# A landing buffer for the gathered tokens: GpSimd copies it to the rows that TensorE turns, and the first two gathers are issued back to back

## The reference

```python
def layer(x, mask, Wq, Wo, ffn):                      # x: 16 x 256 x 512 f32
    h = attention(x, mask, Wq, Wo)                    # 8 heads over 512 positions, rows h: 4096 tokens x 512
    logits = einsum('bsh,eh->bse', h, gate_w); probs = softmax(logits)
    top_w, top_i = top_k(probs, 2); top_w /= sum(top_w)            # 8 experts, 2 for each token
    g = einsum('bsh,ehi->besi', h, w_gate); u = einsum('bsh,ehi->besi', h, w_up)      # I = 352
    expert_out = einsum('besi,eih->besh', silu(g) * u, w_down)
    moe_out = einsum('besh,bse->bsh', expert_out, combine)          # combine: top_w at top_i, else 0
    shared_out = (silu(h @ sw_gate) * (h @ sw_up)) @ sw_down        # 1408 wide
    return x + moe_out + shared_out * sigmoid(h @ shared_gate_w)
```

## Time and profile before

| | |
|---|---|
| median of 3 timed runs | 1990.24 us (1988.90 to 1992.98) |
| the profiled execution | 2000.18 us, of which span 1998.40 us |
| granted TensorE clock, mean | 0.969 |
| TensorE busy in the span | 1887.1 us (94%) |
| VectorE / ScalarE / GpSimd busy | 982.0 / 735.2 / 665.2 us |

### The profile page before, as it was taken

One profiled execution on the slowest core, in us unless ns is written; L12 is line 12 of the kernel. 1 busy time (PEld: TensorE's weight loads), 2 busy tenths in 40 slices (PEclk: granted clock), 3 DMA queues, 4 the chain that ended last, 5 costly groups with the idle time before them and its releaser, 6 DMA issues. The chain is left out here.

```text
span 1998.4 us, 27812 instructions
## 1 busy us (share of the span) xinstructions
PE 1887.1 (94%) x9512; PEld 1382.3 (69%) x9513; DVE 982.0 (49%) x1605; ACT 735.2 (37%) x1432; POOL 665.2 (33%) x500
## 2 busy tenths in 40 slices
PE   4999999999999859799999999989999999999999
PEld 2444444445444347698988999968788888888887
DVE  3677777777777438432333323245523233333333
ACT  1566667666666622343333433331001010101010
POOL 3576776767775616311111111111101001010100
PEclk7899999999999969999999999989999999999999
DMA  6786767676765063433333232253503021211111
GB/s 123 113 134 102 116 100 131 102 116 99 134 91 76 22 217 108 152 117 117 117 117 117 73 119 77 79 184 90 170 31 95 22 84 31 73 42 63 42 43 42
DMA packets 117636, 193.89 MB, mean 97 GB/s; under 512 B 11856, under 2 KB 43600, under 8 KB 117552
## 3 DMA queue, kind: packets, MB, share of 16 engines
q1 hardware_dynamic: 106912, 157.93, 35.3%
q0 software_dynamic: 10640, 34.87, 6.0%
HBM read 99.40 MB, written 42.21 MB: 71 GB/s over the span
## 5 line engine op out<-in xcount | busy, mean ns | idle before, releaser
L382 DVE TENSOR_REDUCE maxcol<-ps_m 128x1 f32<-128x512 f32 x512 | 342.5, 684 | 180.4 <-PE ps_m L525 173.4
L321 ACT ACTIVATE e<-ps_e 128x512 f32<-128x512 f32 x512 | 297.4, 596 | 191.1 <-PE ps_e L520 190.3
L126 POOL TENSOR_TENSOR e<-e 128x2048 f32<-128x2048 f32 x64 | 225.1, 3517 | 99.1 <-ACT e L321 99.1
L1416 ACT ACTIVATE s_silu<-s_ps_g 128x512 f32<-128x512 f32 x77 | 46.0, 598 | 560.9 <-PE s_ps_g L1539 560.9
L1384 POOL DMA_INDIRECT s_chosen<-routed,s_slot_now x64 | 63.4, 991 | 565.8 <-DVE s_total L1470 555.2
L520 PE MATMUL ps_e<-qside,kside 98*128 98x512 f32 x512 | 241.8, 475 | 9.2 <-ACT e L321 7.4
L1495 DVE TENSOR_TENSOR s_h_f<-s_silu,s_ps_u 128x512 f32<-128x512 f32 x77 | 53.0, 688 | 394.2 <-PE s_ps_u L1539 365.8
L520 PEld LDWEIGHTS ps_e<-qside,kside 98*128 98x128 f32 x512 | 96.4, 189 | 213.1 <-ACT e L321 175.4
L525 PE MATMUL ps_m<-kside,qside 97*128 97x512 f32 x512 | 215.3, 424 | 17.7 <-DMA qside<-row_mask 14.2
L1054 DVE TENSOR_TENSOR e_h_lo<-e_ps_h,e_h_hi 128x256 fp32r<-128x256 f32 (+1 forms) x136 | 41.9, 350 | 222.3 <-ACT e_h_hi L869 222.3
L1551 PE MATMUL s_ps_y<-s_d_hi,s_h_hi 128*128 128x512 f32 x352 | 137.8, 392 | 2.5 <-DVE s_h_lo L1452 1.9
(11 more groups left out here) (241 smaller groups left out, 3919.3 us busy)
## 6 DMA issues: line engine op xcount, KB each, us to landing
routed<-keep_y SPq DMA_DIRECT2D x68, 256.0 KB, 2.0
kside<-q_hi SPq DMA_DIRECT2D x64, 256.0 KB
qside<-qm_hi SPq DMA_DIRECT2D x64, 256.0 KB
x_f<-in_x SPq DMA_DIRECT2D x16, 512.0 KB, 4.0
kside<-q_lo SPq DMA_DIRECT2D x32, 256.0 KB
qside<-qm_lo SPq DMA_DIRECT2D x32, 256.0 KB
attn<-xo SPq DMA_DIRECT2D x32, 256.0 KB, 3.9
keep_rows<-attn SPq DMA_DIRECT2D x8, 1024.0 KB, 5.6
```

The lines of the kernel that those rows point to most:

```text
L126: eng.tensor_tensor(into, into, e[k + 1][:, heads, :], ALU.add).then_inc(done, 1)
L321: act.activation(e[kb][:, g, :], ps_e[g % 2][:, :], ACT.Exp, scale=SCALE).then_inc(e_done, 1)
L382: dve.reduce_max(maxcol[par][:, g * KB + kb:g * KB + kb + 1], ps_m[g % 2][:, :], AX.X).then_inc(max_done, 1)
```

## The change

A second buffer of the same size, `landing`, and a second one-column tile, `first_now`, are added. Gather 0 goes straight to `rows`, with its own token column `first_now` and semaphore `first_in`. Gather 1 is issued right behind it, to `landing`. In the loop, GpSimd runs `take(j)`: it waits until gather j has landed and tile j-1's rows have been turned, copies `landing` to `rows` and raises `rows_done`; it then waits for that copy and issues gather j+1 to `landing`. So the data that TensorE turns comes from a copy, not from the DMA; `turn` waits for `rows_done` (for `first_in` at tile 0). The number of gathers is the same, 69; 68 copies of 128 x 512 f32 are added on GpSimd.

```diff
--- before.py
+++ after.py
@@ -586,8 +586,8 @@
     hi = [[sb(f"hi_{w}{n}", raw[k].shape, f32r) for k, w in enumerate("gud")] for n in range(2)]
     lo = [[sb(f"lo_{w}{n}", raw[k].shape, f32r) for k, w in enumerate("gud")] for n in range(2)]
     token_of = sb("token_of", [P, NCOL], u32)
-    now = sb("now", [P, 1], u32)
-    rows = sb("rows", [P, H], f32)
+    first_now, now = sb("first_now", [P, 1], u32), sb("now", [P, 1], u32)
+    rows, landing = sb("rows", [P, H], f32), sb("landing", [P, H], f32)
     x_hi, x_lo = sb("x_hi", [P, HT, ST], f32r), sb("x_lo", [P, HT, ST], f32r)
     silu, h_f = sb("silu", [P, I], f32), sb("h_f", [P, I], f32)
     h_hi, h_lo = sb("h_hi", [P, NI, ST], f32r), sb("h_lo", [P, NI, ST], f32r)
@@ -630,7 +630,7 @@
     row_hot, col_hot, token_hot, id_mm, ids_done = (sem(n) for n in ("row_hot", "col_hot", "token_hot", "id_mm", "ids_done"))
     base, consts, raw_in = sem("base"), sem("consts"), sem("raw_in")
     hi_done, lo_done = sem("hi_done"), sem("lo_done")
-    now_done, rows_in = sem("now_done"), sem("rows_in")
+    now_done, first_in, rows_in, rows_done = sem("now_done"), sem("first_in"), sem("rows_in"), sem("rows_done")
     t_mm, g_mm, half_u, u_mm, ht_mm, y_mm = (sem(n) for n in ("t_mm", "g_mm", "half_u", "u_mm", "ht_mm", "y_mm"))
     xhi_done, xlo_done = sem("xhi_done"), sem("xlo_done")
     silu_done, h_done, hhi_done, h_split = sem("silu_done"), sem("h_done"), sem("hhi_done"), sem("h_split")
@@ -797,21 +797,26 @@
         pool.wait_ge(bounds_done, 1)
         pool.wait_ge(ids_done, 1)
 
-        def gather(j):
-            pool.tensor_copy(now[:], token_of[:, bass.ds(j, 1)]).then_inc(now_done, 1)
-            if began(j):
-                alone(pool, t_mm, 2 * j, ids_done, 1)
+        def gather(j, into, by, landed):
+            pool.tensor_copy(by[:], token_of[:, bass.ds(j, 1)]).then_inc(now_done, 1)
             alone(pool, now_done, j + 1, ids_done, 1)
-            pool.indirect_dma_start(out=rows[:], out_offset=None, in_=attn,
-                                    in_offset=bass.IndirectOffsetOnAxis(ap=now[:, 0:1], axis=0)).then_inc(rows_in, 16)
-
-        gather(0)
+            pool.indirect_dma_start(out=into[:], out_offset=None, in_=attn,
+                                    in_offset=bass.IndirectOffsetOnAxis(ap=by[:, 0:1], axis=0)).then_inc(landed, 16)
+
+        def take(j):
+
+            pool.wait_ge(rows_in, 16 * j)
+            alone(pool, t_mm, 2 * j, ids_done, 1)
+            pool.tensor_copy(rows[:], landing[:]).then_inc(rows_done, 1)
+
+        gather(0, rows, first_now, first_in)
+        gather(1, landing, now, rows_in)
         total = tiles_in_all(pool)
-        with pool.Fori(0, total) as j:
-
-            pool.wait_ge(rows_in, 16 * (j + 1))
-            gather(j + 1)
-        pool.wait_ge(rows_in, 16 * (total + 1))
+        with pool.Fori(1, total) as j:
+            take(j)
+            alone(pool, rows_done, j, ids_done, 1)
+            gather(j + 1, landing, now, rows_in)
+        take(total)
 
     @block.scalar
     def _(act):
@@ -1132,7 +1137,10 @@
         pe.sem_inc(y_mm, 1)
 
         def turn(j):
-            pe.wait_ge(rows_in, 16 * (j + 1))
+            if began(j):
+                pe.wait_ge(rows_done, j)
+            else:
+                pe.wait_ge(first_in, 16)
             for a in range(2):
                 for m in range(HT // 2):
                     k = a * HT // 2 + m
```

## The result

| | before | after |
|---|---|---|
| median of the timed runs (11 each) | 1993.08 us | 1983.49 us |
| lowest to highest | 1988.90 to 1996.03 | 1977.83 to 1987.55 |
| the profiled execution | 2000.18 us | 1980.60 us |
| turn 0 to turn 68 in it | 479.2 us | 466.3 us |

A forecast was written before the change was run, and what follows sets the result against it. TensorE was taken to bound the expert stage, stopped by late gathers and slowed in clock after some stops. Gains 11.4 + 4.8 + 3.9 - 1.4 = 18.7 us, from 1990.24 to 1971.5 us; range 1965 to 1981.

The forecast's parts named there:

- slow tiles: Expert tiles at TensorE's lower clock after three of the six later stops: all three vanish, 3 x 1.6 = 4.8 us gained.
- the first two gathers: First tiles: early gather 1 removes the 5.69 us stop, a new 3 us stop and slow clock follow; gain 3.9 us.
- VectorE beside the copy: Next expert's weight splits on VectorE slowed by GpSimd's copy, once for each of seven experts: loss 1.4 us (0 to 3.6).
- The stops: Steady expert tiles: TensorE's six later waits for gathers vanish, 10.1 us plus 1.3 us lost around them, gain 11.4 us.
- the margin of 9.3 us: Steady tiles: time from a gather's issue to its needed landing with the new buffer, where 5.2 us were; covers 8.0 us gathers.
- nothing in that chain moves: Ordinary tile: the chain through h_lo to TensorE's weight load, with 0.79 us of slack, stays as it was.
- Rival 4: Every tile: the copy holds up VectorE's h_lo, 0.5 us over the slack, 34 us against a gain of 20; 2004 us, chance 0.07.
- Rival 1: First tiles: gather 2 passes the loads in 4 us, so turn 2 has no stop; 1965.5 to 1967 us, chance 0.14.
- Rival 2: Expert tiles: a stop stays at each expert, or only short stops go; gain 8 to 14, about 1979 us, chance 0.12.
- Rival 3: Timed runs: the stops could be the profiler's, so the time stays within 0.2%; chance 0.04.

The follow-up runs named there:

- e7: Changed kernel with new tensors allocated last, next stage's first loads moved to the second last expert, and the copy after h_lo: ratio 0.9934 to before, median 1977.06 us.
- e4: Changed kernel, with GpSimd also waiting for VectorE's h_lo of the same tile before its copy: ratio 0.9939 to the kernel before.
- e2: Changed kernel, with first_now and landing allocated behind all other tensors of the stage: ratio 0.9931 to the kernel before.
- e1: Kernel before, with first_now and landing allocated in their places but never used: ratio 1.0015 to the kernel before.
- e6: Kernel before, with only the 4-byte first_now allocated, unused: profiled only, ordinary tile 6.76 us, turn 0 to turn 68 476.1 us.
- e9: Kernel before, with both new tensors allocated unused, the first 64 bytes instead of 4: profiled only, ordinary tile 6.70 us, turn 0 to turn 68 477.9 us.
- e3: Changed kernel, with the next stage's first loads (2.6 MB) moved from the start of the tiles to the second last expert: ratio 0.9945 to the kernel before.
- e8: Changed kernel, with GpSimd waiting for turn 0 before it issues gather 1: ratio 0.9978 to the kernel before.

## Why the prediction was half right

The sign and the mechanism were right: the landing buffer takes the stops out. Wrong were three terms of the sum, which together are most of what is missing. In the means of the profiles (three before, two after), between turns 0 and 68:

| term | forecast | measured |
|---|---|---|
| stops at turns 13 to 48, with the loss around them | 9.8 | 9.6 |
| the stop at turn 5 | 1.6 | 0.6 |
| slow tiles | 4.8 | 2.6 |
| the first two gathers | 3.9 | 3.4 |
| VectorE beside the copy | -1.4 | -2.6 |
| the pace of TensorE | nothing | -3.2 |
| sum | 18.7 | 10.4 |

The timed medians give 9.6. How the right column comes about: without any stop turns 5 to 68 would have taken 57 x 6.70 + 6 x 7.05 = 424.2 us before, and e7, which has none there, takes 424.18. The three profiles have 436.4 in the mean, 12.2 more; 1.7 slow tiles of 1.56 us over their pace are 2.6 of that, and 9.6 are left for the stops. The changed kernel has 430.0, 5.8 over 424.2: 2.6 come back with e4 (the splits), 3.2 with e2 (the addresses). Turns 0 to 5 went from 40.0 to 36.0, of which 3.4 up to turn 4 and 0.6 from there to turn 5.

**The stops (11.4 us): right, but for one.** GpSimd's round was even shorter than reckoned (copy 0.61, not 0.9; gather issued 1.94 us after the turn, not 2.3). The step that failed here is the word "six": the margin of 9.3 us was worked out for a GpSimd that is on time. At expert 2's loads it was not. Gathers 2 and 3 had landed late, and a round of GpSimd that waits for its own gather takes 841.43 - 836.14 = 5.3 us (gather 4 to gather 5), so that it makes up only 1.5 us with each tile. Gather 5 was issued at 841.43, behind the first of expert 2's loads, and not at about 837.4, 1.94 us behind turn 3, and took 7.8 us. Turn 5 stopped 1.33 us in one profile and 0.52 in the other.

**The slow tiles (4.8 us): the term that was mis-sized.** I counted three of them in one execution and credited them as a fixed cost. In three profiles there were 3, 2 and 0, a mean of 1.7, or 2.6 us. The warning was in my own text: the profiled execution was 9.9 us above the timed median, and I carried the gain over to that median in full.

**The pace: a term that was missing, taken as nothing.** 3.2 us were lost (e2), because even the 4-byte tensor moves the operands of TensorE off their 64-byte starts (e1, e2, e6, e9). No rival held it; "nothing in that chain moves" looked at the order of instructions and not at where their tensors lie.

**VectorE beside the copy (loss 1.4): right, but too small.** The bound from the earlier trace rows, 0 to 0.51 each, held: at the same addresses a split tile takes 7.44 in the changed kernel and 7.01 to 7.03 in e1, and 7.46 in e2 against 7.05 before, 0.41 to 0.43 for each of six, the wait of 0.41 us in the rows above. With the copy moved away (e4) it came back, and the splits and the copy had their old lengths. The Trainium skill's rule ("GPSIMD Engine Reference", Key points: contention where VectorE has two SBUF inputs) puts the loss there too, and the trace of e4 agrees: 1.81 us without the copy beside it, against 2.23. Rival 4, the same in every tile, is refuted: in ordinary tiles h_lo keeps its 0.62 us, and with the addresses put right (e2) the period is 6.70. (Its written sum, 0.75 + 0.62 + 0.7, makes 2.07; the 1.3 that it goes on with is the copy's end at 1.51 less the 0.2 at which `h_lo` starts.)

**The start (3.9 us): near, and partly by luck.** Gather 1 came without a stop, and a new stop stood at turn 2: 2.59 us where 3.0 were forecast. Turn 2 comes 12.5 us after turn 0 (829.6 - 817.0 = 12.6 were forecast). But the 1.6 us that were taken off for a slow clock behind this stop did not come: the granted clock from turn 2 to turn 3 is 1.00 (826.12 to 834.83). What took their place is the stop at turn 3, "nothing, or under 1 us" in the forecast and 1.72 and 1.95 us in the two profiles. One error stood in for another.

Rival 1 (the first stop goes as well) is refuted by the 2.59 us, and e3 shows that even with the next stage's loads gone gather 2 takes 7.0 us. It did get through before the loads were over: it was copied at 825.45, and the DMA engines stayed full until about 834. Rival 2 had about the right size, a gain of 8 to 14, by the wrong mechanism: no stop stays at each expert. Rival 3 falls with the ratio: the timed runs gained what the means of the profiles gained.

## What to carry to other kernels

A second buffer is worth the waits of the slow gathers and no more; count those from several executions, since the length of a stop and what follows it (here zero to three slow-clock tiles, 0 to 5 us) change from one to the next. When a change adds even a four-byte tensor, ask what is allocated behind it: put new small tensors last, or pad them, and compare the period of an undisturbed tile before and after. A copy on GpSimd was free beside VectorE's operations with a PSUM input (`h_lo` 0.62 us with it and without), and belongs outside the stretch in which VectorE subtracts two SBUF tensors.

## What the runs showed of the hardware

- TensorE's pace depends on where its SBUF operands begin: 6.70 us for a tile of 40 matmuls and transposes with tensors at multiples of 64 bytes, 6.76 at 32 over it, the mean of ten tiles in a row the same within 0.005 us in all 14 profiles. The starts are my reading of compiled kernels, not of a trace. In the gate and down products the operands that moved are those of the LDWEIGHTS.
- Two stops of nearly the same length (1.98 and 2.02 us) were followed by an 8.31 us tile at a granted clock of 0.80 and by a 6.77 us tile at 1.00. Of 13 stops of 1.95 to 2.35 us 10 were followed by a slow tile, of 30 of 0.91 to 1.92 us none.
- A GpSimd copy of 128x512 f32 in SBUF took 0.61 us, and up to 1.09 beside two-input VectorE subtractions (minimum, median and maximum of 68 in ns; 1.32 at most in e3 and e8):

```profile
L810 POOL COPY e_rows<-e_landing x68: 610/612/1089, 816.3 to 1273.9; 128x512 f32<-128x512 f32 x68
```

- A 256 KB gather beside 2.1 MB of weight loads took 7.0 us from issue to use even when the further loads were gone (e3), against 3.4 from issue to landing at the median.
